# Attention in a two-layer convolution kernel: scores from stacked 96-row operands, exponentials in groups of three units

## The chip, the cores and the metric

One core of a Trainium2 chip. The metric is the device time of one execution in microseconds. Its engines are named as the profile names them: PE (matrix products; PEld is its weight load), ACT (activation functions), DVE (vector arithmetic), POOL and SP (here both issue DMA transfers). SBUF is the on-chip memory of 128 partitions, PSUM the eight banks of 128 x 512 f32 that PE writes.

## The reference, cut to what matters

Input x is (2, 256, 64, 64), so 2 images of 256 channels and N = 4096 positions.

```python
# layer 0: self-attention, 8 heads of d = 32 channels
qkv = jnp.einsum('oc,bchw->bohw', w_qkv, x)
q, k, v = map(reshape, jnp.split(qkv, 3, axis=1))          # (b, 8, 32, 4096)
scores = jnp.einsum('bhdi,bhdj->bhij', q, k) / jnp.sqrt(jnp.asarray(d, x.dtype))
attn = jax.nn.softmax(scores, axis=-1)
out = jnp.einsum('bhij,bhdj->bhdi', attn, v)
x = jnp.einsum('oc,bchw->bohw', w_proj, out.reshape(b, c, h, w)) + x
# layer 1: a non-local block; 64 channels give theta, 192 give phi (pooled 2x2), all give g (pooled)
f = jnp.einsum('bnc,bcm->bnm', theta_x, phi_x)             # 4096 x 1024
y = jnp.einsum('bnm,bmc->bnc', jax.nn.softmax(f, axis=-1), g_x)
x = batch_norm(_conv1x1(y, W_w, W_b)) + x
```

All is f32. The change touches layer 0 alone.

## The kernel before, in words

For each image the kernel works through two groups of G = 4 heads (128 channels each) and then the second layer: project[0], attend[0], project[1], attend[1], layer1 (lines 1211 to 1291). Every engine has its own program in this order; semaphores tie them together.

*Projection* (`projection`, line 278). Queries, keys and values of one head group from x, in chunks c of 512 positions (NC = 8). x is split into an f16 high and low part (Xh, Xl), and three products hi*hi, lo*hi, hi*lo are summed in PSUM. ACT writes the high half of Q and K (L349), DVE the low half (L379, semaphore s_ev), so that Q and K lie in SBUF as 128 rows (4 heads x 32) by 2 halves by 4096. ACT also squares them (L353) for a bound on the scores, and writes V in f32 (L355). SP does nothing here.

*Attention* (`attention`, line 392). A block is one chunk c of 512 queries; it passes over JT = 32 tiles j of 128 keys. For one tile:

- Scores (L434): `TERMS` gives three rounds (hi*hi, hi*lo, lo*hi), in each round one matmul per head with that head's 32 rows, 128 key columns and 512 queries. The profile writes this shape 32*128: four row tiles of PE side by side. Head 0 goes to the bank `lead` (psO), heads 1 to 3 to one of two sets of three banks.
- Exponentials: ACT reads `lead` (L516, 512 columns) and the three banks (L517, 1536 columns), and writes P, a ring of RING = 8 tiles of 4 x 512 f32.
- Values (L445): out = V^T P in f32 for each head with 128 rows and 32 columns, the shape 128*32: four column tiles side by side, one for each head, all into the bank `both` (psL). They run in halves of 256 columns if need be; `halves_by` says how many halves are done at which tile. Each f32 matmul is two instructions.
- Sums: the softmax's denominators. DVE adds 24 of the 32 tiles of P to `acc` (L561; the last add in two halves, L556 and L558). For the eight tiles in SUM_D, POOL issues transfers that add them to `accD` (L584 the first, L587 the others, two per tile). At a block's border PE multiplies accD and acc with ones (`sums_of_dma` L420, `sums_of_acc` L412) into the same bank, after DVE has copied the values out (L522); DVE then copies the sums out (L530). SP brings them to Ls (L600), DVE inverts them (L564), SP writes them to HBM (L603).

PE computes the scores of tile n+2 (LAG = 2) once `lead` of tile n+1 has been read, then the values of an earlier tile. ACT waits before each tile until the slot of eight tiles ago is free (`slot_free`, line 495): its values computed, and its sum added by DVE or landed by POOL's transfer. Each engine's queue is in order.

*The second layer* (`second_layer`, line 610) starts with the reciprocals of the sums, brought by SP (L1138 broadcasts rows from HBM, L1164 and L1166 move small rows within SBUF). L748 and L779 are f32 matmuls, L760, L775, L828, L829 f16, all in the shape 128*128; L838 and L851 are its main loop. SP issues L175 (loads of x, 512 KB each), L224 (eight small transfers at the start), L1175 (output).

## Time and profile before

| | us |
|---|---|
| median of 3 runs | 2516.49 (2513.29 to 2516.5) |
| profiled execution: span on the page | 2517.7 |
| PE busy | 2451.0 (97%) |
| ACT busy | 2261.4 (90%) |
| DVE busy | 2155.3 (86%) |
| POOL busy | 455.4 (18%) |

The page gives no other time for the profiled execution than its span; the runs of the table are other executions. The engines' busy times overlap. The durations of matmuls are modelled and overlap one another, so PE's busy time isn't PE's work; what a sequence of matmuls costs is read from the distance of their starts. The page's chain, followed back from the end, gives ACT 55%, PE 21% and DVE 14% of the span.

### The profile page before, as it was taken

Reading aid. Unit: us, or ns where it says so; the run is one execution under the profiler, and the core shown is the slowest. Engines: PE = TensorE matmul, PEld = TensorE weight load, DVE = VectorE, ACT = ScalarE, POOL = GpSimd, SP = SyncE. Lnnn points to the kernel's source line nnn. Section 1 sums busy time; section 2 is a strip of 40 time slices with the busy share of each in tenths; the row PEclk is TensorE's granted clock in tenths of the full one; section 3 lists DMA queues with packets and bytes.
Section 4 is the critical chain, followed back from the end, with each engine's and each line's share of the span. In section 5 each row is a group of like instructions: output and inputs, shape, how many; then the busy total and the mean of one; then the engine's idle time right before and its main releaser. Section 6 shows DMA issues by size and latency. Waiting matters only on the chain.

```text
span 2517.7 us, 62570 instructions
## 1 busy us (share of the span) xinstructions
PE 2451.0 (97%) x27104; PEld 783.8 (31%) x27108; DVE 2155.3 (86%) x1386; ACT 2261.4 (90%) x2510; POOL 455.4 (18%) x652
## 2 busy tenths in 40 slices
PE   8999999999999999999999999999999999999998
PEld 3222222242222222344442222222422222223443
DVE  6899999978999999895578999999799999998954
ACT  7999999989999999666489999999899999995663
POOL 0222222202222222110012222222022222220200
PEclk9999999999999999999999999999999999999999
DMA  3777777726777777302237777777177777772011
GB/s 118 147 145 144 147 147 143 147 51 135 148 146 146 146 147 146 92 1 73 82 71 147 148 142 148 147 143 148 43 146 144 148 144 146 147 144 64 1 60 42
DMA packets 96406, 300.38 MB, mean 119 GB/s; under 512 B 18704, under 2 KB 19792, under 8 KB 95856
## 3 DMA queue, kind: packets, MB, share of 16 engines
q0 software_dynamic: 73728, 268.47, 53.2%
q1 hardware_dynamic: 22400, 27.92, 3.4%
q8 instruction: 210, 3.44, 0.6%
q14 instruction: 68, 0.56, 0.1%
HBM read 18.95 MB, written 8.68 MB: 11 GB/s over the span
## 4 chain that ended last, share of the span: by engine, by line
ACT 55%; PE 21%; DVE 14%; issue 6%; DMA 2%; ACTq 0%; POOL 0%; DVEq 0%; SPq 0%; POOLq 0%
ACT arena L517 36%; ACT arena L516 18%; DVE arena L561 10%; PE psOL L851 7%; PE scores L308 3%; DMA arena<-arena 2%; PE psOL L445 2%; PE psOL L775 1%; PE scores L319 1%; PE psOL L434 1%; PE scores L838 1%; PE scores L839 1%; PE scores L828 1%; PE scores L829 1%; DVE arena L1003 1%
## 5 line engine op out<-in xcount | busy, mean ns | idle before, releaser
L561 DVE TENSOR_TENSOR arena<-arena 128x2048 f32<-128x2048 f32 x704 | 1613.4, 2292 | 99.1 <-ACT arena L517 39.8
L517 ACT ACTIVATE arena<-scores 128x1536 f32<-128x1536 f32 x1024 | 1553.6, 1517 | 0.0
L445 PE MATMUL psOL<-arena 128*32 128x512 f32 (+1 forms) x11264 | 1078.9, 484 | 3.0 <-ACT arena L517 1.4
L434 PE MATMUL psOL<-arena 32*128 32x512 f16 x3072 | 835.6, 377 | 12.3 <-ACT arena L516 10.9
L434 PE MATMUL scores<-arena 32*128 32x512 f16 x9216 | 842.6, 378 | 0.0
L516 ACT ACTIVATE arena<-psOL 128x512 f32<-128x512 f32 x1024 | 669.4, 654 | 3.4 <-PE scores L434 3.4
L587 POOL DMA_DIRECT2D arena<-arena x448 | 387.6, 889 | 1136.5 <-ACT arena L517 840.8
L434 PEld LDWEIGHTS psOL<-arena 32*128 32x128 f16 x3072 | 206.3, 92 | 826.0 <-ACT arena L516 706.1
L445 PEld LDWEIGHTS psOL<-arena 128*32 128x32 f32 x11264 | 267.9, 108 | 518.7 <-issue 431.1
L434 PEld LDWEIGHTS scores<-arena 32*128 32x128 f16 x9216 | 220.0, 92 | 0.0
L851 PE MATMUL psOL<-arena 128*128 128x512 f16 x768 | 172.0, 382 | 0.0
L584 POOL DMA_DIRECT2D arena<-arena x64 | 35.2, 556 | 592.5 <-ACT arena L517 592.5
L1115 DVE SCALAR_TENSOR_TENSOR arena<-O,arena 128x1536 f16<-128x1536 f32 (+1 forms) x48 | 75.9, 1581 | 70.3 <-ACT arena L961 66.4
L954 ACT ACTIVATE O<-scores 128x1536 f32<-128x1536 f32 (+1 forms) x48 | 62.4, 1300 | 75.8 <-PE scores L839 75.8
L851 PEld LDWEIGHTS psOL<-arena 128*128 128x128 f16 x768 | 75.6, 98 | 92.1 <-issue 2.7
L933 ACT ACTIVATE arena<-scores,arena 128x1024 f32<-128x1024 f32 x64 | 71.1, 1112 | 26.8 <-POOL arena L719 25.5
L308 PE MATMUL scores<-arena,wq_hi 128*128 128x512 f16 x256 | 71.9, 383 | 10.7 <-DVE wq_lo L243 8.5
L1101 DVE TENSOR_REDUCE arena<-scores 128x1 f32<-128x1024 f32 x64 | 77.9, 1221 | 4.9 <-PE scores L829 3.0
L891 ACT ACTIVATE arena<-X 128x512 f16<-128x512 f32 x32 | 20.1, 630 | 57.4 <-DVE X L997 57.4
L530 DVE COPY L<-psOL 128x512 f32<-128x512 f32 x32 | 22.1, 691 | 53.5 <-PE psOL L412 53.4
L961 ACT ACTIVATE arena<-O 128x1536 f16<-128x1536 f32 (+1 forms) x48 | 64.4, 1341 | 2.8
L349 ACT ACTIVATE arena<-scores 128x1024 f16<-128x1024 f32 x32 | 32.7, 1021 | 37.8 <-PE scores L308 37.8
(120 smaller groups left out, 1419.1 us busy)
## 6 DMA issues: line engine op xcount, KB each, us to landing
arena<-arena POOLq DMA_DIRECT2D x512, 512.0 KB, 5.3
X<-in_x SPq DMA_DIRECT2D x16, 512.0 KB, 5.3
out<-arena SPq DMA_DIRECT2D x32, 256.0 KB, 2.0
arena<-att_inv SPq DMA_DIRECT2D x16, 256.0 KB
arena<-pool_inv SPq DMA_DIRECT2D x2, 2048.0 KB, 7.1
arena<-in_w_qkv SPq DMA_DIRECT2D x1, 768.0 KB, 4.4
Ls<-L SPq DMA_DIRECT2D x32, 8.0 KB
att_inv<-Ls SPq DMA_DIRECT2D x32, 8.0 KB
```

The source lines that it names most:

```text
L308: last = nc.tensor.matmul(slot(w), wq[wp][:, t, outs], xp[:, t, c * CH:(c + 1) * CH], start=(n == 0 and t == 0), stop=(n == 2 and t == CT ...
L434: last = nc.tensor.matmul(dst[h], K[rows, kp, j * 128:(j + 1) * 128], Q[rows, qp, cs], start=(n == 0), stop=(n == 2))
L445: last = nc.tensor.matmul(both[h * D:(h + 1) * D, lo:hi], V[:, j, h * D:(h + 1) * D], P[:, r + h, lo:hi], start=(j == 0), stop=(j == JT - 1))
L516: nc.scalar.activation(P[:, r, :], lead, ACT.Exp, scale=SCORE).then_inc(s_exp, 1)
L517: nc.scalar.activation(P[:, r + 1:r + G, :], bank[n % 2].rearrange("p (u n) -> p u n", n=CH), ACT.Exp, scale=SCORE).then_inc(s_exp, 1)
L561: nc.vector.tensor_tensor(acc[:], old, P[:, r:r + G, :], ALU.add).then_inc(s_add, 1)
L587: nc.gpsimd.dma_start(dst, src, accum_op=ALU.add).then_inc(s_dma[k], 16)
L851: last = nc.tensor.matmul(psOL[:, t * CH:(t + 1) * CH], w[:, m, ts], v[:, p, m, :], start=(n == 0), stop=(n == 3 * MT - 1))
L933: nc.scalar.activation(junk[:, i % 2, :], two_banks(i), ACT.Exp, bias=stat[:, 0, i:i + 1], scale=SCORE1, accum_out=l1[:, i:i + 1]).then_in ...
L961: nc.scalar.activation(Ph[:, p, ms, :], P32[:, p, ms, :], ACT.Copy, scale=PS).then_inc(s_h, 1)
L1101: nc.vector.tensor_reduce(mx[:, i:i + 1], two_banks(i), AX.X, ALU.max).then_inc(s_mx, 1)
L1115: nc.vector.scalar_tensor_tensor(out=Pl[:, p, ms, :], in0=P32[:, p, ms, :], scalar=PS, in1=Ph[:, p, ms, :], op0=ALU.mult, op1=ALU.subtract ...
```

## The change

- K is stored as KS: for each head 96 rows (hi, hi, lo, of 32 rows each), Q as QS2: (hi, lo, hi), one chunk of 512 queries in each of two buffers. One matmul over 96 rows gives the sum of the three products. For one head and one tile (a unit of 512 columns) there are four matmuls of 32 key columns each, in the shape of the values.
- To get there, ACT and DVE write each chunk's halves to one of two buffers `staged`, and SP copies them (`projection.sync`): per chunk 12 transfers for K, one that writes Q to an array q_parts in HBM, and for chunks 0 and 1 another 12 for Q. ACT waits with a chunk until the transfers of two chunks ago landed, and before unit 12 of the attention for all of them. For later blocks SP reloads QS2 from q_parts, three transfers each.
- The exponentials take units in groups of GROUP = 3 (1536 columns) across the borders of tiles; `lead` is gone.
- psO and psL take the values of a block by turns; `acc` has two buffers; the border's sums come three and six groups after the block's last, and DVE copies them at its sixth add.
- The ring has 24 units, which is 6 tiles for 8; the views in `arena` are moved.

```diff
--- before.py
+++ after.py
-RING = 8
-LAG = 2
+GROUP = 3
+RING = 24
 SUM_D = [2, 6, 9, 13, 16, 20, 23, 27]
 SUM_V = [j for j in range(JT) if j not in SUM_D]
 ADDS = len(SUM_V) - 1
-PV_FROM = 2
-PV_MORE = [8, 14, 20, 26]
+UNITS = NC * JT * G
+GROUPS = -(-UNITS // GROUP)
+
+
+def group_size(k):
+
+    return min(GROUP, UNITS - k * GROUP)
+
+
+def exps_through(c, j):
+
+    return ((c * JT + j) * G + G - 1) // GROUP + 1
...
-def halves_by(i):
-
-    return sum(3 if k in PV_MORE else 2 for k in range(PV_FROM, i + 1))
+def halves_by(k):
+
+    if k == GROUPS - 1:
+        return 2 * NC * JT
+    halves = min(k * GROUP // 2, 2 * (min((k + 1) * GROUP, UNITS) // G))
+    return halves - (halves % (2 * JT) in (1, 2 * JT - 1))
...
+        SECOND_AT = 48 * KB
+        RING_AT = 56 * KB
         LATE = 82 * KB
-        Q = view(0, (1, 2, N), F16)[:, 0]
-        K = view(16 * KB, (1, 2, N), F16)[:, 0]
-        V = view(32 * KB, (1, JT, G * D))[:, 0]
-        QK = view(0, (2, 2, N), F16)
-        Xh = view(RING_AT, (1, CT, N), F16)[:, 0]
-        Xl = view(RING_AT + 16 * KB, (1, CT, N), F16)[:, 0]
-        sq = [view(80 * KB + 2 * KB * k, (1, 2, CH), BF16)[:, 0] for k in range(2)]
-        most = view(84 * KB, (1, 2, CH), BF16)[:, 0]
-        top = view(86 * KB, (1, 1, CH), BF16)[:, 0, 0]
-        P = view(RING_AT, (1, RING * G, CH))[:, 0]
-        acc = view(RING_AT + 64 * KB, (1, G, CH))[:, 0]
-        accD = view(RING_AT + 72 * KB, (1, G, CH))[:, 0]
-        wq32 = view(RING_AT + 40 * KB, (1, CT, 3 * C))[:, 0]
-        cw32 = view(RING_AT + 48 * KB, (1, CT, CM + CM + C))[:, 0]
+        SUMS_AT = RING_AT + 2 * KB * RING
+        KS = view(0, (1, G, N), F16)[:, 0]
+        QS2 = [view(32 * KB + 4 * KB * k, (1, G, CH), F16)[:, 0] for k in range(2)]
+        V = view(40 * KB, (1, JT, G * D))[:, 0]
+        Xl = view(RING_AT, (1, CT, N), F16)[:, 0]
+        sq = [view(RING_AT + 16 * KB + 2 * KB * k, (1, 2, CH), BF16)[:, 0] for k in range(2)]
+        most = view(RING_AT + 20 * KB, (1, 2, CH), BF16)[:, 0]
+        top = view(RING_AT + 22 * KB, (1, 1, CH), BF16)[:, 0, 0]
+        staged = [view(RING_AT + 24 * KB + 4 * KB * k, (2, 2, CH), F16) for k in range(2)]
+        Xh = view(RING_AT + 32 * KB, (1, CT, N), F16)[:, 0]
+        P = view(RING_AT, (1, RING, CH))[:, 0]
+        acc = [view(SUMS_AT + 8 * KB * k, (1, G, CH))[:, 0] for k in range(2)]
+        accD = view(SUMS_AT + 16 * KB, (1, G, CH))[:, 0]
+        wq32 = view(SUMS_AT, (1, CT, 3 * C))[:, 0]
+        cw32 = view(SUMS_AT + 8 * KB, (1, CT, CM + CM + C))[:, 0]
+        q_dram = nc.dram_tensor("q_parts", (2, 128, N), F16, kind="Internal").ap()
...
+            s_st = [sem(root, f"s_stacked{k}_{g}") for k in range(2)]
+
+            def stacked(c):
+
+                return 16 * (1 + 6 * G + (1 + 3 * G) * (c // 2))
...
+                    if c >= 2:
+                        act.wait_ge(s_st[c % 2], stacked(c - 2))
+                    nc.scalar.activation(staged[c % 2][:, :, 0, :], both_units(c), ACT.Copy, scale=1.0 / WS
+                                         ).then_inc(s_hi, 1)
                     if c >= 2:
                         act.wait_ge(s_nx, max(1, c - 2))
                     act.wait_ge(s_hi, c + 1)
-                    nc.scalar.activation(sq[c % 2], QK[:, :, 0, cs], ACT.Square).then_inc(s_sq, 1)
+                    nc.scalar.activation(sq[c % 2], staged[c % 2][:, :, 0, :], ACT.Square).then_inc(s_sq, 1)
...
+            def sync(sp):
+                for c in range(NC):
+                    cs = slice(c * CH, (c + 1) * CH)
+                    sp.wait_ge(s_ev, c + 1)
+                    for h in range(G):
+                        heads_rows = slice(h * D, (h + 1) * D)
+                        for r, part in enumerate((0, 0, 1)):
+                            sp.dma_start(KS[r * D:(r + 1) * D, h, cs], staged[c % 2][heads_rows, 1, part, :]
+                                         ).then_inc(s_st[c % 2], 16)
+                        if c < 2:
+                            for r, part in enumerate((0, 1, 0)):
+                                sp.dma_start(QS2[c][r * D:(r + 1) * D, h, :], staged[c][heads_rows, 0, part, :]
+                                             ).then_inc(s_st[c], 16)
+                    sp.dma_start(q_dram[:, :, cs].rearrange("s p n -> p s n"), staged[c % 2][:, 0, :, :]
+                                 ).then_inc(s_st[c % 2], 16)
+
...
             def tensor(pe, free):
-                def scores(c, j):
-
-                    cs = slice(c * CH, (c + 1) * CH)
-                    rest = bank[(c * JT + j) % 2]
-                    dst = [lead] + [rest[:, k * CH:(k + 1) * CH] for k in range(G - 1)]
-                    if c == 0 and j % 4 == 0:
-                        pe.wait_ge(s_ev, j // 4 + 1)
-                    for n, (kp, qp) in enumerate(TERMS):
-                        for h in range(G):
-                            rows = slice(h * D, (h + 1) * D)
-                            last = nc.tensor.matmul(dst[h], K[rows, kp, j * 128:(j + 1) * 128], Q[rows, qp, cs],
-                                                    start=(n == 0), stop=(n == 2))
+                def scores(k):
+                    for i in range(group_size(k)):
+                        n, h = divmod(k * GROUP + i, G)
+                        c, j = divmod(n, JT)
+                        if h == 0 and c == 0 and j % 4 == 0:
+                            pe.wait_ge(s_st[j // 4 % 2], stacked(j // 4))
+                        if h == 0 and j == 0 and c == 1:
+                            pe.wait_ge(s_st[1], stacked(1))
+                        if h == 0 and j == 0 and c >= 2:
+                            pe.wait_ge(s_q[c % 2], 48 * (c // 2))
+                        for m in range(4):
+                            last = nc.tensor.matmul(bank[k % 2][m * D:(m + 1) * D, i * CH:(i + 1) * CH],
+                                                    KS[0:3 * D, h, j * 128 + m * D:j * 128 + (m + 1) * D],
+                                                    QS2[c % 2][0:3 * D, h, :], start=True, stop=True)
                     last.then_inc(s_ready, 1)
 
-                def values(c, j, lo, hi):
-                    if j == 0 and lo == 0 and c:
-                        pe.wait_ge(s_l_free, c)
-                    if j == 0 and lo == 0 and c == 0:
+                def values(n, lo, hi):
+                    c, j = divmod(n, JT)
+                    if j == 0 and lo == 0 and c >= 2:
+                        pe.wait_ge(s_l_free, c - 1)
+                    if j == 0 and lo == 0 and c == 1:
                         pe.wait_ge(s_b, 3)
-                    r = (c * JT + j) % RING * G
+                    r = n * G % RING
                     for h in range(G):
-                        last = nc.tensor.matmul(both[h * D:(h + 1) * D, lo:hi], V[:, j, h * D:(h + 1) * D],
+                        last = nc.tensor.matmul(both(c)[h * D:(h + 1) * D, lo:hi], V[:, j, h * D:(h + 1) * D],
                                                 P[:, r + h, lo:hi], start=(j == 0), stop=(j == JT - 1))
                     if hi == CH:
                         last.then_inc(s_pv, 1)
 
                 if free:
                     pe.wait_ge(*free)
-                keep_busy(both, 7)
+                keep_busy(guard, 7)
                 pe.wait_ge(s_ev, NC - 1)
                 pe.wait_ge(s_ve, NC - 1)
-                scores(0, 0)
-                keep_busy(both, 3)
+                scores(0)
+                keep_busy(guard, 3)
                 pe.wait_ge(s_ev, NC)
                 pe.wait_ge(s_ve, NC)
-                for n in range(1, LAG):
-                    pe.wait_ge(s_exp, 2 * n - 1)
-                    scores(0, n)
-                for n in range(NC * JT):
-                    c, i = divmod(n, JT)
-                    if n + LAG < NC * JT:
-
-                        pe.wait_ge(s_exp, 2 * (n + LAG) - 1)
-                        scores(*divmod(n + LAG, JT))
-                    else:
-                        pe.wait_ge(s_exp, 2 * n + 2)
-                    if n == 0:
+                scores(1)
+                for k in range(GROUPS):
+                    pe.wait_ge(s_exp, k + 1)
+                    if k + 2 < GROUPS:
+                        scores(k + 2)
+                    if k == 0:
                         pe.wait_ge(s_nx, NC)
-                        nc.tensor.matmul(both, heads[:], top, start=True, stop=True).then_inc(s_tr, 1)
-                    if n == 1:
+                        nc.tensor.matmul(guard, heads[:], top, start=True, stop=True).then_inc(s_tr, 1)
+                    if k == 2:
                         pe.wait_ge(s_b, 2)
                         pe.wait_ge(s_id, 2)
-                        nc.tensor.transpose(both[0:1, 0:128], bound[:, 2:3], ident[:, :]).then_inc(s_tr, 1)
-                    if i == 0 and c:
-                        sums_of_dma(pe, c - 1)
-                    if i == 1 and c:
-                        sums_of_acc(pe, c - 1)
-                    at, end = halves_by(i - 1), halves_by(i)
+                        nc.tensor.transpose(guard[0:1, 0:128], bound[:, 2:3], ident[:, :]).then_inc(s_tr, 1)
+                    for c in range(NC - 1):
+                        if k == exps_through(c, JT - 1) + 3:
+                            sums_of_dma(pe, c)
+                        if k == exps_through(c, JT - 1) + 6:
+                            sums_of_acc(pe, c)
+                    at, end = halves_by(k - 1) if k else 0, halves_by(k)
                     while at < end:
-                        j, odd = divmod(at, 2)
+                        n, odd = divmod(at, 2)
                         if odd or at + 1 == end:
-                            values(c, j, odd * CH // 2, (odd + 1) * CH // 2)
+                            values(n, odd * CH // 2, (odd + 1) * CH // 2)
                             at += 1
                         else:
-                            values(c, j, 0, CH)
+                            values(n, 0, CH)
                             at += 2
 
...
-                for m in range(NC * JT - RING, NC * JT - RING + 5):
+                for m in range(NC * JT - RING // G, NC * JT - RING // G + 2):
                     slot_free(act, m)
 
             def scalar(act):
-                for n in range(NC * JT):
-                    r = n % RING * G
-                    act.wait_ge(s_ready, n + 1)
-                    if n >= RING:
-                        slot_free(act, n - RING)
-                    nc.scalar.activation(P[:, r, :], lead, ACT.Exp, scale=SCORE).then_inc(s_exp, 1)
-                    nc.scalar.activation(P[:, r + 1:r + G, :], bank[n % 2].rearrange("p (u n) -> p u n", n=CH),
+                for k in range(GROUPS):
+                    u, size = k * GROUP, group_size(k)
+                    act.wait_ge(s_ready, k + 1)
+                    if u == 6:
+                        act.wait_ge(s_nx, NC)
+                    if u == 12:
+                        for c in (NC - 2, NC - 1):
+                            act.wait_ge(s_st[c % 2], stacked(c))
+                    for m in range(u, u + size):
+                        if m % G == 0 and m >= RING:
+                            slot_free(act, (m - RING) // G)
+                    nc.scalar.activation(P[:, u % RING:u % RING + size, :],
+                                         bank[k % 2][:, 0:size * CH].rearrange("p (u n) -> p u n", n=CH),
                                          ACT.Exp, scale=SCORE).then_inc(s_exp, 1)
 
             def output_out(dve, c):
                 dve.wait_ge(s_pv, (c + 1) * JT)
-                nc.vector.tensor_copy(O[:, g, c * CH:(c + 1) * CH], both).then_inc(s_o_free, 1)
+                nc.vector.tensor_copy(O[:, g, c * CH:(c + 1) * CH], both(c)).then_inc(s_o_free, 1)
 
...
                 for c in range(NC):
-                    if c:
-                        sums_out(dve, c - 1)
                     for n in range(ADDS):
+                        if n == 5 and c:
+                            sums_out(dve, c - 1)
                         j = SUM_V[n + 1]
-                        dve.wait_ge(s_exp, 2 * (c * JT + j) + 2)
-                        r = (c * JT + j) % RING * G
+                        dve.wait_ge(s_exp, exps_through(c, j))
+                        r = (c * JT + j) * G % RING
+                        new = acc[c % 2]
...
+                    if c + 2 < NC:
+                        cs = slice((c + 2) * CH, (c + 3) * CH)
+                        sp.wait_ge(s_ready, exps_through(c, JT - 1))
+                        sp.wait_ge(s_st[c % 2], stacked(c + 2))
+                        for r, part in enumerate((0, 1, 0)):
+                            sp.dma_start(QS2[c % 2][r * D:(r + 1) * D, :, :],
+                                         q_dram[part, :, cs].rearrange("(h d) n -> d h n", d=D)
+                                         ).then_inc(s_q[c % 2], 16)
...
+                    project[0].sync(sp)
                     attend[0].sync(sp, b)
                     if b:
                         sp.wait_ge(s_clean, CLEAN * b)
                         sp.sem_inc(s_past, 1)
+                    project[1].sync(sp)
                     attend[1].sync(sp, b, lambda sp: layer1.signals["rows"](sp, b))
```

## Rows read from the trace of the kernel before

**Rows 1.** The page: span, then busy us, share, instructions of three engines.

```profile
span 2517.7 us, 62570 instructions
...
PE 2451.0 (97%) x27104; PEld 783.8 (31%) x27108; DVE 2155.3 (86%) x1386; ACT 2261.4 (90%) x2510; POOL 455.4 (18%) x652
```

**Rows 2.** The page's groups: busy, mean ns, idle before and its releaser.

```profile
L517 ACT ACTIVATE arena<-scores 128x1536 f32<-128x1536 f32 x1024 | 1553.6, 1517 | 0.0
...
L516 ACT ACTIVATE arena<-psOL 128x512 f32<-128x512 f32 x1024 | 669.4, 654 | 3.4 <-PE scores L434 3.4
```

**Rows 3.** Timeline of ACT in a block: start, duration in us.

```profile
195.49 0.61 ACT L516 ACTIVATE arena<-psOL 128x512 f32<-128x512 f32 x1
195.97 1.47 ACT L517 ACTIVATE arena<-scores 128x1536 f32<-128x1536 f32 x1
197.30 0.63 ACT L516 ACTIVATE arena<-psOL 128x512 f32<-128x512 f32 x1
197.78 1.50 ACT L517 ACTIVATE arena<-scores 128x1536 f32<-128x1536 f32 x1
```

**Rows 4.** Timeline of SP's queue (SPq), two blocks' first transfers.

```profile
228.89 0.55 SPq L600 DMA_DIRECT2D Ls<-L  x1
...
287.79 0.55 SPq L600 DMA_DIRECT2D Ls<-L  x1
```

**Rows 5.** Timeline of PE (matmuls), three tiles; its values' weight loads on the page.

```profile
202.41 1.50 PE L445 MATMUL psOL<-arena 128*32 128x512 f32 x16
203.84 0.39 PE L434 MATMUL psOL<-arena 32*128 32x512 f16 x1
...
204.60 1.07 PE L445 MATMUL psOL<-arena 128*32 128x256 f32 x16
205.60 0.39 PE L434 MATMUL psOL<-arena 32*128 32x512 f16 x1
...
L445 PEld LDWEIGHTS psOL<-arena 128*32 128x32 f32 x11264 | 267.9, 108 | 518.7 <-issue 431.1
```

**Rows 6.** Timelines of DVE and ACT, second projection: first subtraction, first exponential.

```profile
525.05 1.23 DVE L379 SCALAR_TENSOR_TENSOR arena<-scores,arena 128x1024 f16<-128x1024 f32 x1 [1.18 <-ACT arena L349]
...
555.91 0.60 ACT L516 ACTIVATE arena<-psOL 128x512 f32<-128x512 f32 x1 [0.97 <-PE scores L434]
```

**Rows 7.** SP's issues: timeline; L175's min/median/max ns; a small transfer's landing (last number).

```profile
9.98 5.03 SPq L224 DMA_DIRECT2D spread<-ones  x8
...
1034.31 13.53 SPq L1138 DMA_DIRECT2D arena<-att_inv  x8
...
1117.41 0.61 SPq L1164 DMA_DIRECT2D arena<-arena  x1
...
L175 SPq DMA_DIRECT2D X<-in_x x16: 434/442/787, 1.3 to 1259.7; - x16
...
arena<-arena SPq DMA_DIRECT2D x4, 4.0 KB, 1.7
```

**Rows 8.** Timeline of PE in the second layer, f32 between f16, one shape.

```profile
1119.66 0.38 PE L829 MATMUL scores<-arena 128*128 128x512 f16 x1
1119.88 1.03 PE L779 MATMUL psOL<-arena 128*128 128x256 f32 x4
1120.74 0.38 PE L828 MATMUL scores<-arena 128*128 128x512 f16 x1
```

**Rows 9.** DVE in a block: timeline of twelve adds; the page's row of L530.

```profile
228.78 28.64 DVE L561 TENSOR_TENSOR arena<-arena 128x2048 f32<-128x2048 f32 x12
...
L530 DVE COPY L<-psOL 128x512 f32<-128x512 f32 x32 | 22.1, 691 | 53.5 <-PE psOL L412 53.4
```

**Rows 10.** POOL's accumulating transfers (line L587), from issue to landing.

```profile
DMA to landing us min/median/max: 4.5/5.4/8.1
```

**Rows 11.** Windows of PE: length, busy, granted clock, DMA share, GB/s.

```profile
1145.00:1150.00 5.00, 2.52 (x9) 0.79 0.67 246
1150.00:1155.00 5.00, 5.00 (x13) 0.52 0.43 180
```

95 lines of the change are left out of this document (49 added, 46 removed).

## The prediction

> **What bounds the kernel now.** I read the page's busy shares first [rows 1]: PE 97%, ACT 90%, DVE 86%. Three engines close to full decide nothing, so the second view is the list of groups [rows 2]: L517, the exponential of three heads' scores, runs 1024 times, once for each key tile of the 32 attention blocks (2 images x 2 head groups x 8 blocks of 512 queries, each 32 tiles), and that is most of the kernel. The third view, ACT's timeline inside a block [rows 3], shows who waits. The starts stand 1.33 and 0.48 us apart, but the durations creep up by 0.03 us per tile and fall back when the next start is late: the starts run ahead of the work. So I count from end to end (start plus duration): 196.10, 197.44, 197.93, 199.28 us: 1.345 us for 1536 columns, 0.49 for 512, 1.835 per tile. 32 of these are 58.7 us; a block takes 58.90 (spacing of its first SP transfer [rows 4]). ACT therefore sets the attention, at 99.6%. The two costs split into 0.835 ns per column and 0.063 us per instruction.
>
> PE is the runner-up [rows 5]. Scores start at 203.84, the values at 204.60 (0.76 us for three rounds of 0.216, four matmuls side by side in each), the next scores at 205.60 (1.00 us for two half sets of 0.43). A pair of switches between the shapes 32*128 and 128*32 costs 0.76-0.65 plus 1.00-0.86, about 0.25 us a tile. At three halves (202.41 to 203.84) it is still only 1.43, so further sets in one shape are free of it.
>
> Between two attentions lies a projection [rows 6]: from the end of the first eviction of its low halves (L379, 525.05+1.23=526.3) to the first exponential (555.91) 29.6 us; there are four such stretches, within 0.1 us of each other. SP issues a single transfer in each but the first.
>
> **The change, part by part.**
>
> *Exponentials.* 128 units of 512 columns per block go in groups of three: 42.67 instructions of 1.345 us, 57.4 us a block against 58.7. Only the fixed 0.063 us of 21.3 instructions goes. If nothing else bound, that is 58.90-57.4 = 1.5 us a block, 48 us in all: the most the attention can give.
>
> *Scores.* Each unit is now four matmuls of 96 rows x 32 columns, side by side: 0.216 us if they run like the four column tiles of the values, so 0.86 us a tile for 0.65, but in one shape with them, so the 0.25 us goes. PE per block: 128x0.216 + 64x0.43 + two sums of 0.86 = 56.9 us. What of f16 next to f32 in one shape? [rows 8] show it at 128*128: L779 (f32) starts 0.22 us after L829 (f16), and L828 (f16) 0.86 us after L779, which is its bare four instructions. So nothing is added; for column tiles no row shows it.
>
> *A rule weighed.* In the values' rows eight loads of 128x32 lie inside each half set of 0.43 us and cost nothing [rows 5]. The Trainium skill (TensorE: Matmul & The Clock Gate, Part 3, The mechanism) says a weight load overlaps a running matmul only when their row groups differ; all four column tiles of the new scores share their rows, so by the rule each unit would pay its loads. The rows of the values speak against it; it has a rival below.
>
> *Border between blocks.* PE's average work per group is 0.65+0.645 = 1.29 us, 0.055 below ACT's 1.345. Scores of group k+2 start when exponential k ends and are ready 0.94 us later (0.65, and what a 0.38 us matmul lasts beyond its 0.216, and the 0.06 from ACT's end to PE's start), so PE may be 0.4 us late. The two sums (two half sets each, 0.86) come three groups apart on top of the values, 1.7 us against 0.4 of room and 0.16 made up: ACT waits about 1.2 us a block. That leaves 57.4+1.2 = 58.6 against 58.90: 0.3 a block, 10 us in 32. Bounds: 48 us gained without this wait; 32x0.9 = 29 lost if the sums cost 0.9 us more.
>
> *DVE.* 22 adds at 28.64/12 = 2.387, two half adds of 1.14, two copies of 0.6 and a reciprocal of 0.2: 56.2 us a block [rows 9]. The wait before L530 (53.5/32 = 1.7 us) goes (second bank, copy moved to the sixth add). In exchange output_out waits for the values of the last tile, which now follow one group later: 1.345+0.65+0.43 less the half add's 1.14, some 1.3 us. 57.5 in the worst case, still under 58.6: nothing.
>
> *Ring of 6 tiles for 8.* The accumulating transfers take a median 5.4 us, at most 8.1 [rows 10]; SUM_D leaves 3 or 4 tiles (5.4 or 7.2 us) between them, 6.4 on average, and a slot is wanted back 6x57.4/32 = 10.8 us after its exponential. About 1 us of room in the tightest places: nothing, up to 2 us a block (60 in all) if landings lengthen by a fifth.
>
> *Stacking.* This is the large term. SP issues per projection, behind each eviction, 4 heads x 3 K pieces = 12, for c=0 and 1 also 12 Q pieces, and one write of q_parts: 25+25+6x13 = 128 transfers. They hang on the path twice. The two staging buffers free only when their pieces landed (ACT waits stacked(c-2)), and ACT stops at unit 12, before its fifth group, until c=7's pieces landed, since the ring's slots 12 to 15 are the staging. DVE, PE and SP's later work stand behind that. The pieces are 32 rows x 1 KB, SBUF to SBUF. Rows of issues [rows 7]: the eight of L224 5.03/8 = 0.63 us, L1164 0.61, L600 0.55 [rows 4], L175 (large, from HBM) a median 0.44, and the eight broadcasts of L1138 13.53/8 = 1.69. I take 0.60, between the SBUF to SBUF rows; ends 0.44 and 1.69. Landing 1.7 us [rows 7]. The chunk's chain (landing 1.7, a copy on ACT and a subtraction on DVE of up to 1.23 each) is 4.2 us, shorter than 13 issues of 7.8, so SP never waits once started. From the first eviction to the fifth group: 128x0.60+1.7 = 78.5 us. Four groups (5.4 us) are done by then, so the attention starts in effect after 73.1 instead of 29.6: 43.5 us lost, 174 in four projections. (At 0.44: 23, 92 in all; at 0.55: 148; at 0.63: 189.)
>
> *A second rule, against this.* The Trainium skill (DMA: Bandwidth & Descriptors, Issuing engines are not separate DMA queues) calls a sequencer's time to initiate a DMA usually small relative to the DMA itself. Here one issue is 0.6 us against 1.7 to landing, so a third of it, and it is serial. By the rule the stacking would hide; that is the third rival.
>
> *Clock.* PE idles some 7 us before the fifth group: c=6 and 7's pieces need 26 issues, 15.6 us, less what overlaps. In the second layer PE was busy 2.52 us of 5, and the next 5 us ran at a granted clock of 0.52, almost all of it at 1.2 instead of 2.4 GHz [rows 11]. At half clock PE needs 2.6 us a group for ACT's 1.345, and after each stall I allow two such groups: 2.5 us, 10 in all; ends 0 and 32 (10 us cold each time).
>
> *The rest* of the added work is covered: three Q reloads a block (1.8 us of SP, some 40 us before the block that needs them), and a wait of ACT at unit 6 (s_nx, set while group 0 runs). The second layer only moves addresses: nothing.
>
> **Sum.** 2517.7 (span of the profiled execution, the only time the page gives) + 174 - 10 + 10 = 2691.7; the median of the runs shown is 2516.5, 1.2 below, so 2690.
>
> **Rivals.**
> 1. *PE takes over.* Loads or the change of type cost in column tiles too: 0.1 us a unit (about one 108 ns load) makes PE 56.9+12.8 = 69.7 a block, 10.8 over 58.90: +346, with the stacking +174: 3035. If each group kept the 0.25 us, 56.9+10.7 = 67.6: +278, 2970. Against: rows 5 and 8. The weight load rule named above would give the first.
> 2. *Cheap issues, full gain.* Issues at 0.44 and no stall at the border: 2517.7+92-48 = 2562. For: L175 [rows 7]. Against: all SBUF to SBUF rows are above 0.54.
> 3. *The stacking hides (faster).* An issue costs little or SP's issues overlap. From 128i+1.7-5.4 = 29.6, below i = 0.26 us, nothing is lost, and the groups' 10 to 48 us stay: about 2480. Against: the cheapest row here is L175's minimum, 0.43. This is the other side, and what the skill's "small" would give.
> 4. *Transfers, not issues.* 128 transfers through one queue take longer than they issue, 0.9 us each: 115-33 = 82 a projection, +328: 2845. For: the eight of L1138 with their 1.69. Against: 32 KB per 0.6 us is 55 GB/s, and POOL's transfers of 512 KB land in 5.4, 97 GB/s [rows 10].
>
> **How the numbers follow.** Forecast 0.72, rivals in order 0.07, 0.10, 0.04, 0.07. Its own range: issues 0.55 to 0.63, 2617 to 2740. I stretch to 2580 for part of rival 2 and to 2780. Only rival 3 is faster by over 0.2% (5 us, what a measurement of this kernel can tell): 0.04; same 0.02; slower 0.94.
>
> **What would show it.** Right: SP's queue full of issues 0.55 to 0.65 apart through each projection, ACT idle before its fifth group, some 44 us more between the attentions, blocks of 58 to 59 us, PE waiting for ACT inside them. Wrong: blocks above 60 (PE or ring), SP idle within the projections while ACT waits for landings, or attentions still 40 us apart.

## The result and the profile after

The changed kernel takes 2833.26 us (median of 4 runs, 2832.05 to 2836.22) against 2516.47 beside it (2513.29 to 2516.5): a ratio of 1.1263 [1.1247, 1.1278]. The direction was forecast; the size was not, +317 us for +174, and the time lies outside the range. The page of the changed kernel, with the columns of [rows 1, 2] (its values at L492 and scores at L479 both stand on column tiles now):

```profile
span 2831.0 us, 74824 instructions
PE 2534.4 (90%) x33248; PEld 1084.0 (38%) x33252; DVE 2153.1 (76%) x1386; ACT 2239.8 (79%) x1830; POOL 456.0 (16%) x652
DMA 29%; PE 24%; ACT 19%; issue 14%; SPq 7%; DVE 5%; POOL 1%; ACTq 0%; POOLq 0%; DVEq 0%
L564 ACT ACTIVATE arena<-scores 128x1536 f32<-128x1536 f32 x1368 | 1863.1, 1477 | 171.2 <-DMA arena<-arena 74.8
L370 ACT ACTIVATE arena<-scores 128x1024 f16<-128x1024 f32 x32 | 32.8, 1024 | 208.5 <-DMA q_parts<-arena 171.0
arena<-arena POOLq DMA_DIRECT2D x512, 512.0 KB, 5.2
```

PE's busy share falls from 97% to 90% and ACT's from 90% to 79%, so neither sets the time by its work, and the chain is led by transfers. The two ACT rows say where the waits are: 208.5 us before an eviction of the projections (L370, 171.0 of them put down to SP's transfers; 37.8 in the kernel before, at L349), 171.2 us before the exponentials (3.4 before), 74.8 of them for landings of the accumulating transfers.

**The projections.** SP's queue through the first of them (start, duration of the issues together, count):

```profile
16.26 1.81 SPq L416 DMA_DIRECT2D arena<-arena  x3
57.07 7.50 SPq L416 DMA_DIRECT2D arena<-arena  x12
65.24 8.14 SPq L416 DMA_DIRECT2D arena<-arena  x12
73.42 0.59 SPq L422 DMA_DIRECT2D q_parts<-arena  x1
90.34 9.14 SPq L416 DMA_DIRECT2D arena<-arena  x12
99.53 0.58 SPq L422 DMA_DIRECT2D q_parts<-arena  x1
```

It never rests: twelve copies take 7.50 us, 0.63 each, and now and then a hitch of 0.6 or 1.6 us is added (8.14, 9.14). From 16.26 to 100.11 us (99.53+0.58) that makes 83.85/128 = 0.655. ACT meanwhile (start, duration, count, idle time before and its releaser):

```profile
87.30 2.78 ACT L564 ACTIVATE arena<-scores 128x1536 f32<-128x1536 f32 x2
90.32 1.45 ACT L564 ACTIVATE arena<-scores 128x1536 f32<-128x1536 f32 x1 [0.23 <-PE scores L479]
92.26 1.45 ACT L564 ACTIVATE arena<-scores 128x1536 f32<-128x1536 f32 x1 [0.49 <-PE scores L479]
101.98 2.79 ACT L564 ACTIVATE arena<-scores 128x1536 f32<-128x1536 f32 x2 [8.27 <-DMA q_parts<-arena]
105.01 1.45 ACT L564 ACTIVATE arena<-scores 128x1536 f32<-128x1536 f32 x1 [0.23 <-PE scores L479]
108.00 1.45 ACT L564 ACTIVATE arena<-scores 128x1536 f32<-128x1536 f32 x1 [1.53 <-PE scores L479]
693.00 2.79 ACT L564 ACTIVATE arena<-scores 128x1536 f32<-128x1536 f32 x2 [8.11 <-DMA q_parts<-arena]
```

Four groups, then the stop before the fifth until the last piece of SP has landed, then a wait of 1.53 us for a slow PE. The windows (length, busy us and count of PE, PEld, DVE, ACT, POOL; granted clock, DMA share, GB/s) show the clock:

```profile
10.00:100.00 90.00, 51.71 (x393) 25.21 (x392) 27.09 (x30) 32.52 (x35) 1.28 (x2) 0.79 0.37 106
100.00:105.00 5.00, 1.51 (x16) 0.68 (x20) 0.19 (x1) 2.79 (x2) 0.00 (x0) 0.50 0.18 59
105.00:110.00 5.00, 5.00 (x48) 1.71 (x44) 4.79 (x3) 3.03 (x3) 0.00 (x0) 0.56 0.00 0
110.00:115.00 5.00, 5.00 (x92) 2.17 (x84) 2.68 (x2) 4.95 (x4) 1.82 (x2) 1.00 0.12 23
```

After the stop PE runs at 0.50, the level of 1.2 GHz, and is back at 1.00 from 110 us on; ACT's wait of 1.53 us for it (1.34 after two of the other stops) lies behind the fifth group. Over the four head groups the attention starts in effect 52.0, 51.4, 48.5 and 52.4 us later than before (for the second: ACT's fifth group at 693.00 less four of 1.345, less the end of the attention before at 596.37, is 91.2, against 39.8 by the same count in the kernel before): 204 us. ACT's own rows say the same: 171 us more before the evictions and 34.6 us of stops before the fifth groups.

**The blocks.** SP's first transfer of each block, for [rows 4]:

```profile
178.78 0.70 SPq L650 DMA_DIRECT2D Ls<-L  x1
...
555.52 0.56 SPq L650 DMA_DIRECT2D Ls<-L  x1
```

From 178.78 to 555.52 are six blocks of 62.8 us, for 58.9. Above 60 us was the prediction's own sign of being wrong. Of the 313.3 us between the two spans the blocks hold what the projections' 204 leave, 109, or 3.4 a block on average over all 32; some 7 us of it are ACT's waits for a slow PE after the four stops. ACT over the third block, and POOL, which issues the accumulating transfers:

```profile
236.37 13.54 ACT L564 ACTIVATE arena<-scores 128x1536 f32<-128x1536 f32 x10 [0.66 <-PE scores L479]
251.32 6.82 ACT L564 ACTIVATE arena<-scores 128x1536 f32<-128x1536 f32 x5 [1.40 <-DMA arena<-arena]
258.55 19.05 ACT L564 ACTIVATE arena<-scores 128x1536 f32<-128x1536 f32 x14 [0.41 <-DMA arena<-arena]
277.76 12.19 ACT L564 ACTIVATE arena<-scores 128x1536 f32<-128x1536 f32 x9 [0.16 <-DMA arena<-arena]
290.14 1.45 ACT L564 ACTIVATE arena<-scores 128x1536 f32<-128x1536 f32 x1 [0.19 <-PE scores L479]
292.09 4.32 ACT L564 ACTIVATE arena<-scores 128x1536 f32<-128x1536 f32 x3 [0.49 <-PE scores L479]
297.05 9.51 ACT L564 ACTIVATE arena<-scores 128x1536 f32<-128x1536 f32 x7 [0.65 <-PE scores L479]
```

```profile
242.15 0.86 POOL L637 DMA_DIRECT2D arena<-arena  x1 [4.35 <-ACT arena L564]
244.24 0.86 POOL L637 DMA_DIRECT2D arena<-arena  x1 [1.23 <-DMA arena<-arena]
```

Two kinds of wait lie on ACT. Three at the border, for PE: 0.19+0.49+0.65 = 1.33 us. And inside the block those for landings (1.40, 0.41 and 0.16 us in this one): the first can be followed through. The tile's exponentials end at about 242.0, POOL issues its first half at 242.15 but the second only at 244.24, since the transfer before it into the same sums had not landed. The slot was wanted back when the tenth group had ended, at 249.91. ACT went on at 251.32, 7.1 us after the second issue; the landings in this stretch take 4.9 to 7.0 us. **The room is thus 249.9-242.0, some 8 us: six groups of 1.345 = 8.07, and not the 10.8 of the prediction.**

### The profile page after: what moved, and what is told of

Its sections match the earlier page's. It is cut to its first block, busy times and chain, and to the rows that moved or that the text cites. A ratio compares the mean times of both kernels' runs of the same rounds, so it can differ in the third digit from the quotient of the medians.

```text
span 2831.0 us, 74824 instructions
## 1 busy us (share of the span) xinstructions
PE 2534.4 (90%) x33248; PEld 1084.0 (38%) x33252; DVE 2153.1 (76%) x1386; ACT 2239.8 (79%) x1830; POOL 456.0 (16%) x652
## 4 chain that ended last, share of the span: by engine, by line
DMA 29%; PE 24%; ACT 19%; issue 14%; SPq 7%; DVE 5%; POOL 1%; ACTq 0%; POOLq 0%; DVEq 0%
DMA arena<-arena 29%; ACT arena L564 18%; PE scores L479 6%; PE psOL L909 6%; SPq L416 5%; PE psOL L492 5%; SPq L420 2%; DVE arena L610 1%; PE psOL L833 1%; PE psOL L463 1%; PE scores L896 1%; PE scores L897 1%; PE scores L886 1%; PE scores L887 1%; POOL arena L637 1%
## 5 line engine op out<-in xcount | busy, mean ns | idle before, releaser
L564 ACT ACTIVATE arena<-scores 128x1536 f32<-128x1536 f32 x1368 | 1863.1, 1477 | 171.2 <-DMA arena<-arena 74.8
L479 PE MATMUL scores<-arena 96*32 96x512 f16 x16384 | 1148.2, 386 | 145.1 <-ACT arena L564 112.1
L492 PE MATMUL psOL<-arena 128*32 128x256 f32 (+1 forms) x13312 | 1129.7, 432 | 1.4 <-ACT arena L564 1.4
L479 PEld LDWEIGHTS scores<-arena 96*32 96x32 f16 x16384 | 382.5, 96 | 874.2 <-ACT arena L564 551.1
L637 POOL DMA_DIRECT2D arena<-arena x448 | 388.2, 903 | 1193.4 <-ACT arena L564 902.2
L492 PEld LDWEIGHTS psOL<-arena 128*32 128x32 f32 x13312 | 402.4, 111 | 377.8 <-issue 54.2
L370 ACT ACTIVATE arena<-scores 128x1024 f16<-128x1024 f32 x32 | 32.8, 1024 | 208.5 <-DMA q_parts<-arena 171.0
L328 PE MATMUL scores<-arena,wq_hi 128*128 128x512 f16 x256 | 89.1, 459 | 117.7 <-ACT arena L357 108.4
L400 DVE SCALAR_TENSOR_TENSOR arena<-scores,arena 128x1024 f16<-128x1024 f32 x32 | 39.2, 1225 | 183.1 <-ACT arena L370 183.1
L1012 ACT ACTIVATE O<-scores 128x1536 f32<-128x1536 f32 (+1 forms) x48 | 62.5, 1301 | 73.0 <-PE scores L897 73.0
L328 PEld LDWEIGHTS scores<-arena,wq_hi 128*128 128x128 f16 x256 | 26.2, 111 | 157.2 <-issue 134.6
L949 ACT ACTIVATE arena<-X 128x512 f16<-128x512 f32 x32 | 20.2, 630 | 56.8 <-DVE X L1055 56.8
L390 DVE SCALAR_TENSOR_TENSOR arena<-X,arena 128x1024 f16<-128x1024 f32 x32 | 39.1, 1224 | 29.7 <-ACT arena L357 29.7
L806 PE MATMUL scores<-O,wp_sb 128*128 128x512 f32 x128 | 58.2, 597 | 0.0
```

Of the source, the lines that this page charges most:

```text
L328: last = nc.tensor.matmul(slot(w), wq[wp][:, t, outs], xp[:, t, c * CH:(c + 1) * CH], start=(n == 0 and t == 0), stop=(n == 2 and t == CT ...
L479: last = nc.tensor.matmul(bank[k % 2][m * D:(m + 1) * D, i * CH:(i + 1) * CH], KS[0:3 * D, h, j * 128 + m * D:j * 128 + (m + 1) * D], QS2[ ...
L492: last = nc.tensor.matmul(both(c)[h * D:(h + 1) * D, lo:hi], V[:, j, h * D:(h + 1) * D], P[:, r + h, lo:hi], start=(j == 0), stop=(j == JT ...
L564: nc.scalar.activation(P[:, u % RING:u % RING + size, :], bank[k % 2][:, 0:size * CH].rearrange("p (u n) -> p u n", n=CH), ACT.Exp, scale= ...
L637: nc.gpsimd.dma_start(dst, src, accum_op=ALU.add).then_inc(s_dma[k], 16)
```

## The experiments

The kernel before ran beside each of them (medians 2514.9 to 2516.0), and every ratio is to it. A block's length is the mean spacing of SP's first transfers in the first attention. Experiments 1, 2, 4 and 13 start from the changed kernel, 3 and 9 from the kernel before, the others from experiment 4; the diffs show the lines that matter, "..." marks what is left out.

**1. No reload of Q** (leaves the reloads out, so blocks 2 to 7 of an attention use the queries of 0 and 1).

```diff
-                        for r, part in enumerate((0, 1, 0)):
-                            sp.dma_start(QS2[c % 2][r * D:(r + 1) * D, :, :],
...
-                            pe.wait_ge(s_q[c % 2], 48 * (c // 2))
```

> Leaves out the three reloads of Q per block, so blocks 2 to 7 of each group work on the queries of blocks 0 and 1. Theory A (the reloads run into POOL's accumulating transfers, whose landings then hold ring slots): ACT's waits for landings inside the attentions fall from 19 us per attention to under 6, blocks from 62.5 to about 60.5, the time to 2770. Theory B (six slots alone are too few, reloads are harmless): waits and blocks stay, 2825 to 2835.

Measured 2798.65 (2794.17 to 2806.17), ratio 1.1125 [1.1101, 1.1150], blocks of the first attention 61.0. That lies between what the two theories expected. The reloads beside the accumulations cost 35 us in all: a third of the blocks' 109, not all of it.

**2. Half of the accumulations** (heads 2 and 3 have only their first copy, so their sums are incomplete).

```diff
+                                if k == 1:
+                                    continue
                                 pool.wait_ge(s_dma[k], 16 * (c * len(SUM_D) + i))
```

> Leaves out the accumulating transfers of heads 2 and 3 but for the first of each block (their softmax sums lack seven tiles). If landings hold the ring's slots (theories A and B alike): no wait of ACT for a landing inside the attentions, blocks 60.0 (57.4 and the border's 1.4, some starts), 2760. Theory C (the wait for landings only covers a wait for PE or DVE that is as long): blocks stay above 62, 2820 or more.

Measured 2723.75 (2723.04 to 2724.78), 1.0825 [1.0807, 1.0843], blocks 59.0: with a median landing of 4.6 us and one transfer at a time, the whole 109 us of the blocks go, 36 us more than expected. ACT in one block, nothing left but the border:

```profile
229.78 49.80 ACT L567 ACTIVATE arena<-scores 128x1536 f32<-128x1536 f32 x37
279.77 1.45 ACT L567 ACTIVATE arena<-scores 128x1536 f32<-128x1536 f32 x1 [0.19 <-PE scores L479]
281.71 4.32 ACT L567 ACTIVATE arena<-scores 128x1536 f32<-128x1536 f32 x3 [0.49 <-PE scores L479]
286.68 13.54 ACT L567 ACTIVATE arena<-scores 128x1536 f32<-128x1536 f32 x10 [0.65 <-PE scores L479]
```

**3. The kernel before with a ring of six**, and nothing else of the change (but for the wait named in the expectation).

```diff
-RING = 8
+RING = 6
```

> The kernel before with a ring of 6 tiles for 8 (and, at the two borders to a second projection, a wait for all six slots, some 3 us each). Theory B: blocks go from 58.9 to 61, 2585. Theory A (reloads needed): blocks 59.0 to 59.5, 2520 to 2540.

Measured 2537.51 (2533.77 to 2540.78), 1.0081 [1.0064, 1.0097], blocks 59.3. Six tiles for eight cost 21 us there, where a slot's room falls from 7 x 1.835 = 12.8 us to 9.2. ACT's waits for landings are 12.1 us of it:

```profile
L516 ACT ACTIVATE arena<-psOL 128x512 f32<-128x512 f32 x1024 | 681.1, 665 | 16.5 <-DMA arena<-arena 12.1 <-PE scores L434 3.4 <-PE psOL L445 0.7
```

About 7 us more are the wait for all slots at the two second projections, which this run and experiments 9 and 10 add (ACT's idle time before L337 is 9.3 us for 2.1). That looked like an acquittal of the ring; it was none, for in the changed kernel the same six tiles leave 8.07 (experiments 9 to 13).

**4. K stacked through HBM**: K's parts are written to HBM and read back in three transfers of 128 KB for each eviction, so that SP issues 46 transfers a projection for 128.

```diff
+                    for r, part in enumerate((0, 0, 1)):
+                        sp.dma_start(KS[r * D:(r + 1) * D, :, cs],
+                                     k_dram[part, :, cs].rearrange("(h d) n -> d h n", d=D)
+                                     ).then_inc(s_kr[c % 2], 16)
...
```

> The changed kernel with K stacked like the reloads of Q: two writes to HBM per chunk and three reads back, 46 transfers issued per projection for 128. If SP's issues set the projection: the distance from the last exponential to the first of the next attention (after the stop) falls from 91 us to 42, four times 49 saved, 2640. Rival (what sets it is the landing of the pieces): writes of 2.4 and reads of 5.5 us are longer than the 1.9 of the direct pieces, so at most half is saved, 2735 or more.

Measured 2624.12 (2619.89 to 2627.59), 1.0430 [1.0412, 1.0447], blocks 62.5. The queue now has gaps between the evictions:

```profile
35.71 0.38 SPq L435 DMA_DIRECT2D q_parts<-arena  x1
36.12 0.47 SPq L435 DMA_DIRECT2D k_parts<-arena  x1
36.70 2.44 SPq L427 DMA_DIRECT2D arena<-k_parts  x3
39.63 0.38 SPq L435 DMA_DIRECT2D q_parts<-arena  x1
```

209 us are saved for the 204 that the projections had lost and the slow PE after the stops, although more bytes move (343.1 MB for 334.8): the number of issues set their length. The edit also lets ACT go on as soon as the two writes of a chunk have landed, so the run alone doesn't tell issues from landings; that the queue never rested in the changed kernel does. That settles the first term and leaves the blocks.

**5 to 8. Four edits at the blocks**, all on top of 4: the tiles that go to the accumulations moved (5, below); 5 with the reload in three pieces spread over the block (6); 5 with no reload (7, leaves it out, as 1 does); 5 with the second border sum in two halves, later (8).

```diff
-            SUM_D = [2, 6, 9, 13, 16, 20, 23, 27]
+            SUM_D = [4, 7, 11, 14, 18, 21, 25, 28]
```

> K through HBM as in the run before, and POOL's eight tiles moved from 2, 6, ... 27 to 4, 7, ... 28, so that the first copy of a block no longer waits for PE's late sums (at the second projection the scalar engine waits for tile 28's transfer, some 2 us twice). If the late first copy sets the chain of landings back: ACT's waits for landings halve, blocks 62.5 to 61.3, 2585. Rival (the chain keeps up after two tiles anyway, only its length and the reloads count): blocks 62.5, 2624.

> The run before it, and the three reloads of Q of a block issued at its tiles 6, 17 and 24 instead of together. If three transfers of 128 KB at once are too much for the one microsecond of room, but one isn't: blocks 0.8 to 1.8 us below those of the shifted kernel, near 60.0, 2545. Rival (each piece costs its share wherever it falls): no gain on the shifted kernel within 5 us.

> The shifted kernel without the reloads of Q (blocks 2 to 7 use the queries of blocks 0 and 1). With late first copy and reload both gone, blocks as with half the sums, 59.0 to 59.4, 2515 to 2530. If six slots alone still cost something: above 59.8.

> The shifted kernel with the border's second sum cut into two halves of 256 columns, 11 and 21 groups after the block's last, for one sum of 512 after six (DVE's copy and reciprocal later by as much). If PE's lateness at the border is what ACT waits for besides landings (1.4 us a block): 0.8 us a block less, 25 us below the shifted kernel. Rival (the wait only moves to the next landing): within 8 us of it.

Measured 2633.67 (2627.40 to 2638.08), 2632.52 (2631.13 to 2645.96), 2610.36 (2604.14 to 2612.02) and 2632.36 (2627.25 to 2638.60); ratios 1.0467, 1.0467, 1.0370 and 1.0468, each within 0.0023. None did what I expected; for 5, 6 and 8 the recorded rivals came within 10 us. A late first copy into the sums is not the cause (5), and even without reloads the first attention's blocks are 61.7 us (7). ACT waits for landings 82.2, 78.0, 52.6 and 75.7 us in 5 to 8, for 70.1 in 4. Two of the edits also paid elsewhere: ACT's wait at the start of the second layer, 56.8 us in 4, is 62.4 in 5 and 70.3 in 8, so that what the split took off ACT's waits in the attention (122.0 us for 136.3) was in good part spent there. What all four share is the six-tile ring asked for by whole tile.

**9. The kernel before with a ring of five** (room 4 x 1.835 = 7.3 us).

```diff
-RING = 8
+RING = 5
```

> The kernel before with a ring of 5 tiles. New theory (the time between a tile's exponential and the wish for its slot decides, and 'six tiles' is less of it than I took: before, ring 8, 7 x 1.835 = 12.8 us; ring 6, 9.2; the changed kernel, whose waits are rounded to groups of three units, 6 groups x 1.345 = 8.1): ring 5 leaves 7.3 us, less than the changed kernel, so blocks 61.5 to 62.5 for 59.4 at ring 6, 2610 to 2640. Rival (something else in the new order of work lengthens the landings): blocks under 60.5, 2580.

Measured 2657.19 (2653.86 to 2659.24), 1.0564 [1.0547, 1.0582], blocks 62.8, more than expected. The row of its wait, for the second of [rows 2]:

```profile
L516 ACT ACTIVATE arena<-psOL 128x512 f32<-128x512 f32 x1024 | 644.8, 630 | 117.6 <-DMA arena<-arena 99.4
```

So, on one and the same kernel, room 12.8, 9.2 and 7.3 us gives 2516, 2538 and 2657 us, with 0, 12.1 and 99.4 us of waits for landings: flat, then steep. The changed kernel, with 8.07 us of room and 74.8 us of waits, stands on the steep part.

**10. A ring of nine tiles** on top of 4 (heads 2 and 3 use the keys of heads 0 and 1, which frees the space, and the accumulations go to an idle part of O; room for a slot 10 groups, 13.4 us).

```diff
-RING = 24
+RING = 36
...
-        KS = view(0, (1, G, N), F16)[:, 0]
+        KS = view(0, (1, 2, N), F16)[:, 0]
...
```

> K through HBM, and a ring of 36 units (9 tiles): heads 2 and 3 use the keys of heads 0 and 1, and POOL's sums lie in an idle part of O, so the second layer's input is spoiled. Room 10 groups = 13.4 us, with all reloads. Room theory: no wait for landings, blocks 59.0 as with half the sums, 2510 to 2520. Rival (reloads and late copies lengthen the chain itself, so that no ring is long enough): blocks above 60.5.

Measured 2533.10 (2529.26 to 2536.74), 1.0068 [1.0051, 1.0084], blocks 59.0. The same accumulations, the same reloads of Q (K's reads in the projections are half as large), and 91 us less than 4: the row of the exponentials has no wait for landings left among its releasers. The time is 13 us above the most that was expected; 11.5 us of it is ACT's wait at the two second projections, where this run asks for all nine tiles.

**11. Waits of two units** on top of 4, ring still six tiles: POOL issues a half when the group that ends its two heads is done, and ACT asks for a slot two units at a time, so the half of heads 2 and 3, which is issued later, is also wanted back later. By the same count each half's room is now 7, 7 and 6 groups by turns, 9.0 us on average. It computes everything.

```diff
-            def slot_free(act, m):
+            def slot_free(act, m, halves=(0, 1)):
...
-                    for k in range(2):
+                    for k in halves:
...
-                            pool.wait_ge(s_exp, exps_through(c, j))
+                            pool.wait_ge(s_exp, ((c * JT + j) * G + 2 * k + 1) // GROUP + 1)
...
-                        if m % G == 0 and m >= RING:
-                            slot_free(act, (m - RING) // G)
+                        if m % 2 == 0 and m >= RING:
+                            slot_free(act, (m - RING) // G, (m % G // 2,))
```

> K through HBM, with the waits at the grain of two units: POOL issues heads 0 and 1 when their group is done, ACT asks for the slots of heads 2 and 3 two units later. Same ring, same traffic. Room theory: about 0.9 us more for each half, blocks 1.0 to 2.0 us shorter, 2565 to 2595. Rival: within 8 us of 2624.

Measured 2537.94 (2537.00 to 2538.50), 1.0093 [1.0076, 1.0110], blocks 59.6: 86 us less than 4 and below what was expected, for three changed waits and no byte less. ACT, idle time before the exponentials by releaser, in 4 and in 11:

```profile
L581 ACT ACTIVATE arena<-scores 128x1536 f32<-128x1536 f32 x1368 | 1861.6, 1478 | 132.6 <-DMA arena<-arena 70.1 <-PE scores L496 53.0 <-PE psOL L509 5.7
```

```profile
L582 ACT ACTIVATE arena<-scores 128x1536 f32<-128x1536 f32 x1368 | 1850.0, 1520 | 56.7 <-PE scores L496 37.9 <-DMA arena<-arena 14.5 <-PE psOL L509 1.6
```

**12. Experiment 11 with the spread reload of 6 and the split sum of 8.**

> The fine waits, the second border sum in two halves and the reloads spread over the block. If waits for landings no longer cover PE's lateness, the border's cut now shows: 10 to 30 us below the fine waits alone, about 2555. Rival (landings still decide): equal to it within 8 us.

Measured 2774.49 (2772.45 to 2778.94), 1.1036 [1.1017, 1.1054], blocks 69.1: 237 us above 11 and far from either theory. SP and PE around a border:

```profile
218.42 0.45 SPq L676 DMA_DIRECT2D arena<-q_parts  x1
234.74 0.57 SPq L681 DMA_DIRECT2D att_inv<-Ls  x1
235.36 0.47 SPq L686 DMA_DIRECT2D arena<-q_parts  x1
235.88 0.43 SPq L692 DMA_DIRECT2D arena<-q_parts  x1
```

```profile
230.53 0.60 PE L510 MATMUL psOL<-arena 128*32 128x256 f32 x8
238.78 1.47 PE L497 MATMUL scores<-arena 96*32 96x512 f16 x12 [7.65 <-DMA arena<-q_parts]
```

The split puts off the inverse (L681), and in SP's queue the second and third piece of the reload now stand behind the wait for it. They are issued at 235.36 and 235.88; PE wanted the queries at 231.1 and got them at 238.78, and went on at half clock (0.50 from 238.7 to 243 us). The next two runs take the pair apart.

**13 to 15.** Run 13 is the changed kernel itself, copies and reloads as they are, with the three waits of 11 alone; 14 is 11 with the split sum, 15 is 11 with the spread reload.

> The changed kernel itself (stacking copies, reloads and ring of 24 units as they are) with one thing added: slots are asked for and accumulations issued two units at a time instead of by whole tile. It computes the full result. Theory (the failed step is the room of the ring, 8.1 us between a tile's exponential and the group that wants its slot): the same edit took 86 us off the kernel with K through HBM; here 70 to 90 us, 2745 to 2765, blocks 59.5 to 60.5 us, the projections still 50 us a head group longer. Rival (the changed kernel's blocks are long by the copies or the clock, not by the slots): 2815 to 2835.

> The kernel with K through HBM and two-unit waits, plus the second border sum in two halves at groups 11 and 21 of the next block; reloads stay in one place, ahead of the wait for the inverse in SP's queue. It computes the full result. Theory 1 (the miss of the run before came from reload pieces queued behind the late inverse, which put PE's first scores of a block 8 us late): no such wait here, and ACT's last border waits, 0.66 us of 1.3 us a block, go: 2515 to 2535. Theory 2 (the late border sum itself costs the 10 us a block, by psOL or DVE): 2700 to 2780.

> The kernel with K through HBM and two-unit waits, plus the reload of Q in three pieces, two of them behind the wait for the inverse, which stands early here. It computes the full result. Theory 1 (only the pair of edits is harmful): 2535 to 2550. Theory 2 (spread pieces are harmful by themselves): 2600 or more.

Run 13: 2742.08 (2741.70 to 2745.30), 1.0904 [1.0886, 1.0922], 91 us below the changed kernel, with blocks of 59.5; its L565 row waits 12.7 us for landings, for 74.8. Time and blocks are at or just past the low edge of what was expected. The failed step is confirmed on the kernel that it was about, and what is left is the projections:

```profile
L370 ACT ACTIVATE arena<-scores 128x1024 f16<-128x1024 f32 x32 | 32.7, 1023 | 207.3 <-DMA q_parts<-arena 170.3 <-PE scores L328 37.0
```

Run 14: 2557.54 (2556.80 to 2564.52), 1.0176 [1.0158, 1.0194]; run 15: 2528.17 (2524.35 to 2533.26), 1.0057 [1.0040, 1.0073]. Neither edit alone costs the 10 us a block of run 12; the pair does, by the queue's order. But theory 1 was wrong of run 14's gain: the split costs 20 us. In the attention it gives and takes: ACT's waits for PE over one border fall to 0.66, 0.19 and 0.19 us, 0.3 less, and it waits more for landings (0.64 us in one block, 1.44 in the next, 22.7 us in all for 14.5 in run 11). Most of the 20 us lie outside it, before the second layer, in run 11 and in run 14:

```profile
L967 ACT ACTIVATE arena<-X 128x512 f16<-128x512 f32 x32 | 20.2, 630 | 56.8 <-DVE X L1073 56.8
L970 ACT ACTIVATE arena<-X 128x512 f16<-128x512 f32 x32 | 20.2, 630 | 71.0 <-DVE X L1076 71.0
```

The late inverse of an attention's last block but one (its transfer is issued at 1044.63 us, for 1016.66 in run 11) holds back the reads of the reciprocals behind it in SP's queue (1046.61 for 1037.91), and with them the second layer: 14 us over two images. This is read from the order of the rows, and no run tests it; why more landings are waited for stays open. Run 15 is the best of all that compute everything, and still 13 us above the kernel before.

## Why the prediction was wrong

**Ring of 6 tiles for 8: the step that failed.** It said "a slot is wanted back 6x57.4/32 = 10.8 us after its exponential", and "nothing, up to 2 us a block". Six tiles is the distance from a slot's exponential to its next one, begin to begin. The transfer can begin only when the whole tile is done, and the slot must be free before the first group that touches its next tile: that takes a tile's length and the rounding to groups off, and leaves 8.07 us. From the rows known then it would have been 8.07-5.4 = 2.7 us over the median landing and none over the maximum of 8.1 [rows 10]; the delay of a second half, 2.1 us here, then takes up the rest. Size: 109 us measured in the blocks (some 7 of it the clock's), 0 forecast, 60 granted at most. The median landing of the accumulating transfers stayed at 5.4 us (L637; its maximum went from 8.1 to 9.0). It was the room that moved, and not the typical landing, but for the reloads' share of experiment 1; experiments 9 to 11 and 13 show it from both sides.

**Stacking: right mechanism, sized low.** 128 issues at 0.655 us, not 0.60: 128 x 0.655 + 1.7 - 5.4 - 29.6 = 50.5, for 51 measured and 43.5 forecast. The hitches in the long runs of twelve account for 0.02 of it, the bare issue at 0.63 for the rest; in four projections 204 us for 174. So of the 139 us that the forecast lacks, 30 are this term and 109 the blocks. Issues of 0.63 (189) and the ring's bound of 60 together would have made 2516.5+189-10+10+60 = 2766, inside the range: with its allowances used up the prediction would still have been 68 us short. Rivals 2 and 3 wanted issues of 0.44 and less; 3 falls with experiment 4: fewer issues and more bytes gave back 209 us. Rival 4 falls too: issue to issue is 0.63, not 0.9, and the stop ends 2.4 us after SP began to issue its last transfer (99.53 to 101.98). Its 2845 lies within 0.5% of the measured time all the same, by luck: the mechanism isn't there. The Trainium skill (DMA: Bandwidth & Descriptors, Issuing engines are not separate DMA queues) calls the time to initiate a transfer usually small relative to the transfer itself. This trace disagrees for transfers of 32 KB, issued in 0.63 us each and landed in a median 1.9: their serial issues held up a projection by 51 us.

**Scores and the change of type: right.** PE inside a block, for [rows 5]:

```profile
242.56 1.04 PE L492 MATMUL psOL<-arena 128*32 128x256 f32 x16
243.43 0.82 PE L479 MATMUL scores<-arena 96*32 96x512 f16 x12
244.08 0.61 PE L492 MATMUL psOL<-arena 128*32 128x256 f32 x8
```

Twelve score matmuls, three units, take 244.08-243.43 = 0.65 us, 0.216 a unit, and the two half sets before them 0.87, as in the kernel before: f16 and f32 by turns in one shape cost nothing, and 12 loads of weights vanish under 12 matmuls. Rival 1 falls. The Trainium skill (TensorE: Matmul & The Clock Gate, Part 3, The mechanism) wants different row groups for such an overlap; all four column tiles share theirs, and the rows go against the rule.

**Exponentials, border, DVE: right in kind, the gain absent.** The border waits are 1.33 us for 1.2. With landings out of the way blocks are 59.0 us (experiments 2 and 10) for a forecast of 58.6 and 58.9 in the kernel before: the grouping gains nothing, where 10 us were forecast and 48 were the most.

**Clock: right.** The granted clock is 0.50 or 0.51 in the 5 us after each of the four stops. ACT waits for a late group 1.53, 1.53, 1.34 and 1.34 us, with the small waits beside it some 7 us in all, for 10.

## What to carry to other kernels

Count a buffer's room from the last event that lets its transfer be issued to the first instruction that asks for it back, with the grain of the waits on both sides taken off; here that grain, three changed waits, was worth 86 to 91 us. Room well above the landing time buys nothing, and near it every microsecond counts (9.2, 8.07 and 7.3 us left ACT waiting 12, 75 and 99 us), so a test in another kernel (experiment 3) must reproduce the room in microseconds and not the number of slots. A data movement cut into many small transfers is priced by its issues in one queue, and what is put in that queue behind a wait inherits that wait.

## What the hardware showed beside that

One 32-row copy occupies SP for 0.63 us, issue to issue, and a plain 256 KB write for 0.41 (35.71 to 36.12): 46 larger transfers through HBM beat 128 small ones inside SBUF by 209 us. And the three reloads a block, of 128 KB in rows of 1 KB, cost 35 us in all, 1.1 a block, though in the 16 us from 240 on their queue moves 0.40 MB against the accumulations' 2.63.
